# Query and key weights of an attention folded into one matrix ahead of time, in a two-layer Perceiver kernel

## The reference, cut to what matters

```python
# L0_ffn (end of the first layer)
h = layernorm(x, ln1_g, ln1_b)
h = bitlinear(h, w1, b1)          # activations rounded to 8 bits per row, weights to -1, 0, 1
h = gelu(h)                       # 1024 wide
h = layernorm(h, ln2_g, ln2_b)
h = bitlinear(h, w2, b2)
x = x + h
# L1_xattn (start of the second layer), q = layernorm(x), k = v = ctx_1024
wq = einsum('bsd,ed->bse', q, Wq) + bq
wk = einsum('bsd,ed->bse', k, Wk) + bk
wv = einsum('bsd,ed->bse', v, Wv) + bv
att_score = einsum('bqd,bkd->bqk', wq, wk) / 16 + att_mask
x = x + einsum('bqk,bkd->bqd', softmax(att_score), wv)
```

## Time and profile before

| | |
|---|---|
| median of 3 runs | 1007.73 us (1007.71 to 1008.43) |
| the profiled execution | 1003.05 us, its span 1001.0 us |
| PE busy in the span | 905.0 us (90%) |
| VectorE, ScalarE, GpSimd busy | 604.5, 479.5, 105.7 us (60%, 48%, 11%) |
| mean granted TensorE clock in the span | 0.964 |

### The profile page before, as it was taken

One profiled execution on the slowest core, in us unless ns is written; L12 is line 12 of the kernel. 1 busy time (PEld: TensorE's weight loads), 2 busy tenths in 40 slices (PEclk: granted clock), 3 DMA queues, 4 the chain that ended last, 5 costly groups with the idle time before them and its releaser, 6 DMA issues.

```text
span 1001.0 us, 15431 instructions
## 1 busy us (share of the span) xinstructions
PE 905.0 (90%) x6066; PEld 540.6 (54%) x6068; DVE 604.5 (60%) x1075; ACT 479.5 (48%) x951; POOL 105.7 (11%) x118
## 2 busy tenths in 40 slices
PE   6786799999999999999998899588999989988788
PEld 3444444444555555455544677354875854555656
DVE  3876577787885447888843586858414127188240
ACT  2232366777775557777788532225213110676111
POOL 1421011111000000000000200101000007155000
PEclk9999899999999999999999999779999989999889
DMA  9772823445323112222522700705438350000000
GB/s 358 218 202 93 259 79 107 133 127 163 101 66 105 33 32 65 64 67 74 191 96 76 261 1 1 253 25 184 163 133 303 118 168 1 1 1 2 0 1 22
DMA packets 68837, 108.70 MB, mean 109 GB/s; under 512 B 7062, under 2 KB 42902, under 8 KB 66838
## 3 DMA queue, kind: packets, MB, share of 16 engines
q1 hardware_dynamic: 67372, 101.92, 32.0%
q10 hardware_dynamic: 1392, 5.77, 1.4%
HBM read 93.77 MB, written 13.89 MB: 108 GB/s over the span
## 4 chain that ended last, share of the span: by engine, by line
PE 79%; DVE 8%; ACT 7%; issue 3%; DMA 2%; SPq 0%; POOL 0%; ACTq 0%; DVEq 0%
PE psum L1803 13%; PE psum L1785 11%; PE psum L1756 10%; PE psum L2172 6%; PE psum L2145 5%; PE psum L1934 5%; PE psum L1738 5%; PE psum L1728 4%; PE psum L2265 4%; PE psum L1947 3%; ACT arena L748 3%; DVE arena L1100 2%; PE psum L2313 2%; PE psum L2401 1%; PE psum L2298 1%
## 5 line engine op out<-in xcount | busy, mean ns | idle before, releaser
L1100 DVE TENSOR_REDUCE arena<-psum 128x1 f32<-128x1024 f32 x256 | 300.5, 1218 | 111.6 <-PE psum L1756 111.5
L748 ACT ACTIVATE arena<-psum 128x512 f32<-128x512 f32 x512 | 264.7, 604 | 63.4 <-PE psum L1785 62.3
L1785 PE MATMUL psum<-arena 99*128 99x256 bf16 x1024 | 161.0, 275 | 10.4 <-ACT arena L748 4.8
L1756 PE MATMUL psum<-arena 96*128 96x512 bf16 x512 | 152.2, 383 | 18.1 <-DVE arena L1100 11.4
L1785 PEld LDWEIGHTS psum<-arena 99*128 99x128 bf16 x1024 | 80.0, 97 | 109.2 <-ACT arena L748 50.6
L1803 PE MATMUL psum<-arena 128*32 128x256 f32 x2048 | 136.8, 385 | 0.0
L1803 PEld LDWEIGHTS psum<-arena 128*32 128x32 f32 x2048 | 53.5, 109 | 75.5 <-ACT arena L748 36.9
L1728 PE MATMUL psum<-arena 128*128 128x512 f32 x128 | 64.2, 630 | 5.6 <-DMA arena<-ctxT 5.6
L1756 PEld LDWEIGHTS psum<-arena 96*128 96x128 bf16 x512 | 49.3, 99 | 35.7 <-DVE arena L1100 18.8
L1738 PE MATMUL psum<-arena 128*128 128x256 f32 x256 | 64.2, 395 | 1.0 <-ACT arena L726 1.0
L647 POOL TENSOR_TENSOR arena<-arena 128x512 bf16<-128x512 f32 x34 | 41.5, 1221 | 210.0 <-DVE arena L1086 202.3
(11 more groups left out here) (241 smaller groups left out, 967.2 us busy)
## 6 DMA issues: line engine op xcount, KB each, us to landing
arena<-kparts SPq DMA_DIRECT2D x192, 128.0 KB, 3.0
kparts<-arena SPq DMA_DIRECT2D x32, 384.0 KB, 3.3
arena<-ctxT SPq DMA_DIRECT2D x21, 512.0 KB, 5.2
arena<-ctx SPq DMA_DIRECT2D x2, 4096.0 KB, 15.3
arena<-mask SPq DMA_DIRECT2D x8, 1024.0 KB, 5.1
arena<-mask ACTq DMA_DIRECT2D x4, 1024.0 KB, 13.4
arena<-ctxT SPq DMA_DIRECT2D x1, 4096.0 KB, 13.7
arena<-ctxT SPq DMA_DIRECT2D x4, 1024.0 KB, 8.6
```

The lines of the kernel that those rows point to most:

```text
L748: nc.scalar.activation(PR[step % 4][:, pair * CH:(pair + 1) * CH], ring_bank(slot), ACT.Exp)\
L1100: nc.vector.tensor_reduce(MX[g % 2][:, col:col + 1], unit_banks(n).rearrange("p b n -> p (b n)"), AX.X, ALU.max).then_inc(s_maxed, 1)
L1756: last = nc.tensor.matmul(out, q, KST[g % 2][0:ROWS, j, at], start=True, stop=not masked, skip_group_check=True)
L1785: last = nc.tensor.matmul(ring_heads(slot)[:, u, :], KST[gg % 2][0:KROWS, j, kc * P:(kc + 1) * P], QST[0:KROWS, G * g + j, b * S:(b + 1) * S],
```

## The change

The product of the query weights with the key weights is made once, on the chip, and the query's normalised tokens are multiplied by that alone. `fold_key_weights` computes WQ1'WK1 (four fp32 products, 256 columns each), the two bias vectors WK1'bq and WQ1'bk (eight products of one column), and the number bq'bk (two of one by one). ScalarE copies them (`copy_key_weights`, four activations). `project_queries` and `copy_queries` go, for both batches. `fold_queries` reads the tokens `HTE` and the folded weights; `copy_folded` gets a bias operand. `bias_queries` reads the tokens and gets one more product per tile, which adds the number: six products in place of four. The query weights are now loaded untransposed, by a DMA of the same size.

```diff
-        QUERY_BANKS = ((0, 1), (7, 3))
         QC_BANKS = ((2, 3), (7, 3))
-        QE = f32(32768, 1024).rearrange("p (c n) -> p c n", c=CT)
+        WQK = f32(32768, 512).rearrange("p (c f) -> p c f", c=CT)
+        FOLDED = f32(33280, 5)
...
-            load(WQ1, by_part("wq1T"), "l1w_loaded")
+            load(WQ1, by_part("wq1"), "l1w_loaded")
...
-            def copy_queries(b):
-                for f in range(CT):
-                    act.wait_ge(on["e_q"], CT * b + f + 1)
-                    signal(nc.scalar.activation(QE[:, f, batch(b)], psum[:, QUERY_BANKS[b][f], 0:S], ACT.Identity,
-                                                bias=col("bq1", f)), "e_q_copied")
+            def copy_key_weights():
+
+                act.wait_ge(on["e_fold"], 1)
+                signal(nc.scalar.activation(WQK.rearrange("p c f -> p (c f)"), psum[:, 0, :], ACT.Copy), "e_folded")
+                signal(nc.scalar.activation(FOLDED[:, 0:2], psum[:, 1, 0:2], ACT.Copy, scale=D ** -0.5), "e_folded")
+                signal(nc.scalar.activation(FOLDED[:, 2:4], psum[:, 1, 2:4], ACT.Copy), "e_folded")
+                signal(nc.scalar.activation(FOLDED[0:1, 4:5], psum[0:1, 1, 4:5], ACT.Copy), "e_folded")
...
-                    signal(nc.scalar.activation(QC[:, c, batch(b)], psum[:, QC_BANKS[b][c], 0:S], ACT.Copy,
-                                                scale=D ** -0.5), "e_qc_copied")
+                    signal(nc.scalar.activation(QC[:, c, batch(b)], psum[:, QC_BANKS[b][c], 0:S], ACT.Identity,
+                                                scale=D ** -0.5, bias=FOLDED[:, c:c + 1]), "e_qc_copied")
...
             centre_odd(0)
+            copy_key_weights()
+            act.wait_ge(on["e_folded"], 4)
             copy_hidden(0)
             copy_hidden(1)
...
-            copy_queries(0)
             copy_folded(0)
...
-            def project_queries(b):
+            def fold_key_weights():
+
+                for c in range(CT):
+                    for f in range(CT):
+                        nc.tensor.matmul(psum[:, 0, c * 256:(c + 1) * 256], WQ1[:, f, c * P:(c + 1) * P], WK1[:, f, :],
+                                         start=(f == 0), stop=(f == CT - 1), skip_group_check=True)
+                for weights, bias, at in ((WK1, "bq1", 0), (WQ1, "bk1", 2)):
+                    for c in range(CT):
+                        for f in range(CT):
+                            nc.tensor.matmul(psum[:, 1, at + c:at + c + 1], weights[:, f, c * P:(c + 1) * P], col(bias, f),
+                                             start=(f == 0), stop=(f == CT - 1), skip_group_check=True)
                 for f in range(CT):
-                    linear(psum[:, QUERY_BANKS[b][f], 0:S], WQ1, [HTE[:, c, batch(b)] for c in range(CT)], f, "e_q")
+                    last = nc.tensor.matmul(psum[0:1, 1, 4:5], col("bq1", f), col("bk1", f), start=(f == 0),
+                                            stop=(f == CT - 1), skip_group_check=True)
+                last.then_inc(on["e_fold"], 1)
 
             def fold_queries(b):
-                pe.wait_ge(on["e_q_copied"], CT * (b + 1))
                 for c in range(CT):
-                    linear(psum[:, QC_BANKS[b][c], 0:S], WK1, [QE[:, k, batch(b)] for k in range(CT)], c, "e_qc")
+                    linear(psum[:, QC_BANKS[b][c], 0:S], WQK, [HTE[:, k, batch(b)] for k in range(CT)], c, "e_qc")
 
             def bias_queries(b):
                 for i in range(2):
-                    for k in range(CT):
-                        last = nc.tensor.matmul(psum[:, CQ_BANK[b], i:i + 1],
-                                                QE[:, k, (2 * b + i) * P:(2 * b + i + 1) * P], col("bk1", k),
-                                                start=(k == 0), stop=(k == CT - 1))
+                    at = slice((2 * b + i) * P, (2 * b + i + 1) * P)
+                    for c in range(CT):
+                        nc.tensor.matmul(psum[:, CQ_BANK[b], i:i + 1], HTE[:, c, at], FOLDED[:, 2 + c:3 + c],
+                                         start=(c == 0), stop=False, skip_group_check=True)
+                    last = nc.tensor.matmul(psum[:, CQ_BANK[b], i:i + 1], ONES[0:1, :], FOLDED[0:1, 4:5],
+                                            start=False, stop=True, skip_group_check=True)
...
             pe.wait_ge(on["d_hidden"], 4)
+            pe.wait_ge(on["l1w_loaded"], 64)
+            fold_key_weights()
             for i in range(2):
                 turn_hidden(i)
                 project_down(i)
...
-            project_queries(0)
+            pe.wait_ge(on["e_folded"], 4)
             fold_queries(0)
...
-            project_queries(1)
             weigh_context(1, 3)
             fold_queries(1)
```

More of the change, by code:

```diff
@@ L398, in build @@
             d_turned2_copied d_down
-            e_q e_q_copied e_qc e_qc_copied e_cq e_cq_copied e_scores e_masked e_bias e_exp
+            e_fold e_folded e_qc e_qc_copied e_cq e_cq_copied e_scores e_masked e_bias e_exp
             e_turned e_turned_a e_turned_v e_att e_normed e_out
@@ L969, in _ @@
             copy_exps(1, 6)
-            copy_queries(1)
             copy_folded(1)
@@ L2128, in _ @@
             pe.wait_ge(on["x_ready"], 2 * TT + 2)
-            pe.wait_ge(on["l1w_loaded"], 64)
             turn_half(HLE, 0, 2 * TT)
             turned()
-            project_queries(0)
+            pe.wait_ge(on["e_folded"], 4)
             fold_queries(0)
@@ L2467, in layout @@
         "w1T": c(a["L0_ffn_w1"].T), "w2T": c(a["L0_ffn_w2"].T),
-        "wq1T": c(a["L1_xattn_Wq"].T), "wk1": c(a["L1_xattn_Wk"]), "wv1T": c(a["L1_xattn_Wv"].T),
+        "wq1": c(a["L1_xattn_Wq"]), "wk1": c(a["L1_xattn_Wk"]), "wv1T": c(a["L1_xattn_Wv"].T),
         "ctx": c(a["ctx_1024"]), "mask1": c(a["mask_SxS2_ff0"]),
```

## The result

The changed kernel takes 1013.47 us (median of 15 runs, 1009.03 to 1015.65), the kernel before 1007.71 in the same comparison (15 runs). The ratio is 1.006 with a 95% interval of [1.004, 1.008]: slower by 0.6%, some 5.8 us, where 1007.1 had been forecast. The profiled execution took 1013.69 us with a span of 1011.9. The page's shares say almost nothing of the reason.

What follows compares the result with a forecast made beforehand. Bound by a chain of waits across engines up to the scores, then by PE nearly alone. Batch 1's half -1.1, batch 0's -2.5, fold +3.0, clock 0: -0.6 on 1007.73, so 1007.1 us; range 1001.8 to 1010.6.

Steps and rivals of the forecast that it cites:

- the second fetch: Behind the branch, in the fold: starts after three records have run, takes 2.56 us, done at 638.9.
- +3.0: Fold behind the branch: copies end at 646.3, where copy_hidden(0) had started at 643.30; taken from bounds -1.1 to +3.0 us.
- The pieces: Fold behind the branch: three records, a fetch stop, then five wide records 2.4 us, sixteen narrow 3.5, and 0.3.
- ScalarE's copies: Four copies of the fold, ahead of copy_hidden(0) in ScalarE's queue: 1.2 us, ending at 646.3, fold ending at 645.1.
- the delay is carried on in full: From copy_hidden(0) to VectorE's sum at 650.16: steps in a row without slack, so all +3.0 us carries on.
- The gain if the stop were gone: At turn_hidden(0): without its stall, tile 1's transposes start at 644.75 and not 645.85, -1.1 us.
- Batch 0's: Batch 0's half at half clock, up to the scores: one projection fewer, twelve narrow records at 2.6 us; -2.5 us.
- Batch 1's: Batch 1's half at full clock: four products go (1.73 us), bias columns +0.5, copy with bias +0.09; -1.1 us.
- The third rival: Batch 1's half: something else ends last there, so its path isn't shortened; sum +0.5, 1008.2 us, chance 0.03.
- the slower rival: Scores: single columns ahead delay the clock's rise, price 1.5 to 4.1, taken 3.4; 1010.5 us, chance 0.22.
- The other reason for taking 0: Clock at the scores: timed runs lie 4.7 us above the profiled one, so its lucky rise need not be theirs.
- The free fold: Behind the branch: fold ends ahead of 641, turn_hidden(0) goes without stall; -4.7, 1003.0 us, chance 0.35.

Runs made afterwards that it cites:

- e7: Changed kernel with the fold put behind project_down(1) and its copies between two of ScalarE's square roots; 1008.1 us, ratio 1.0028 to the kernel before.
- e6: Kernel before, without the change, its 6 MB mask and context loads held back until tile 1 is rounded; 1004.39 us, ratio 0.9983.
- e1: Kernel before plus the fold and its copies behind the branch, results unused, queries still projected twice; 1012.22 us, ratio 1.0060.
- e2: Changed kernel with PE's part of the fold moved ahead of the branch, behind the mixer's last product; 1008.09 us, ratio 1.0017 to the kernel before.
- e4: Changed kernel with the If's two arms exchanged, so PE falls through into the fold without a taken branch; 1012.29 us, ratio 1.0084 to the kernel before.
- e3: Changed kernel with the 6 MB mask and context loads held back until tile 1 is rounded; 1002.32 us, ratio 0.9976 to the kernel before.
- e8: Changed kernel with the fold ahead of the branch and the mask and context loads held back; 1002.21 us, ratio 0.9956 to the kernel before.
- e11: Changed kernel with the fold ahead of the branch and batch 0's bias columns behind unit 0's scores; 1002.71 us, ratio 0.9981 to the kernel before.
- e9: Changed kernel with fold ahead of the branch, loads held back and batch 0's bias columns behind unit 0's scores; 1003.12 us, ratio 0.9965 to the kernel before.

## Why the prediction was wrong

**The step that failed is the second fetch.** The prediction had it start "on demand" after three records and take 2.56 us, as the first. Its length was nearly right: from the packet to the next record it was 2.67 and 2.52 us here. What was wrong is when it starts. PE wanted it at 641.90, and the packet came at 644.58, 6.24 behind the first. So the code is complete 9.0 us after the mixer's end (638.06 to 647.10), and it was so before (633.64 to 642.55: 8.9). Before, 6.25 of these lay under PE's wait for VectorE, so the stop read 2.18, which was only the part that stuck out. That the second packet fell beside the start of the transposes, 639.98 and 639.89, was a coincidence (and again in e7): in e6 it came 5.65 us ahead of them, and in the changed kernel 2.7 us behind the point where PE needed it. The two packets of the earlier trace rows, 6.3 us apart, were the evidence, and I read them as two separate demands. With 9.0 us and then 5 wide and 16 narrow records and four more, 5.9 us at half clock, the fold ends 15 us after the mixer, and nothing of that piece has cover: +6.3 us instead of +3.0. Of these 3.3 us the code's coming makes 3.8 (9.0 us after the mixer's end in place of the 5.3 of the forecast); the rest of the fold took 0.3 less than reckoned, and the way from it to `copy_hidden(0)` 0.1 less. e1, e2, e4 and e7 show that it is the place behind a taken branch; e3 that the load on the DMA engines nearly doubles the distance of the two pages there.

**The pieces.** Three records, then five, with an "issue" between them: right. Durations of the fold at half clock: 2.50 for five wide records (2.4 forecast), 3.21 for sixteen narrow (3.5): right. ScalarE's copies were forecast to end 1.2 us behind the fold and to push `copy_hidden(0)`. They end under the transposes, at 653.7, and L908 starts at 654.03, right behind the turning, so they cost nothing. That the sum lost little by this is luck: from the fold's end to `copy_hidden(0)` it had 1.2 us for the copies and nothing for the transposes, and the transposes took 1.06:

```profile
653.01 0.60 ACT L920 ACTIVATE arena<-psum 128x512 f32<-128x512 f32 x1 [14.02 <-PE psum L2042]
...
654.03 1.02 ACT L908 ACTIVATE arena<-psum 128x1024 bf16<-128x1024 bf16 x1 [0.29 <-PE psum L2022]
```

**That the delay is carried on in full**: right, 6.3 at `copy_hidden(0)` and at the sum. (The gain if the stop were gone, put at 1.1 us, measured 1.4: the sum at 9.00 in e4, e6 and e8.) It was the step that turned an error of 3.3 us at the fetch into one of 3.3 in the whole.

**The halves.** Batch 0's -2.37 (forecast -2.5, with the twelve narrow records at 2.6 measured as 0.65 + 0.51 + 0.94 + 0.51 = 2.61). Batch 1's -0.86 (forecast -1.1; the twelve narrow records took 1.76, from 751.07 to 752.83, where 1.58 was reckoned). The third rival falls.

**The clock.** I took 0 and made it the slower rival, at 1.5 to 4.1 us. It cost +2.5 under the scores, and the dip at 889 goes with the last +0.9. As an effect the rival was right, and the three pairs with the columns moved speak for its mechanism, as far as said above. Its price would not have saved the number: -0.6 + 3.3 for the fetch + 2.5 + 0.9 + 0.4 for the halves gives the 6.5 of the table. The range ended at 1010.6, since it added the clock to a +3.0 that was given as an upper bound. That bound was none: it held only if the second fetch starts when PE asks. The other reason for taking 0, the 4.7 us between the timed runs and the profiled one, fits the lower clock near 560 us, far ahead of the change, and says nothing of the rise before the scores. (Added up from their pieces the chances come to 0.42 for the same and 0.21 for slower, where the text has 0.41 and 0.22; nothing hangs on it.)

**The free fold**, the first rival, fails here for the same reason, but e2 shows that the fold is free directly ahead of the branch, though the stop at `turn_hidden(0)` stays.

**The rule.** The Trainium skill, "Runtime: NRT & Kernel Launch", "Instruction fetch mechanics", says that a taken branch outside the held pages forces a fetch and that fetching in sequence is mostly hidden. The measurement decides against the second half behind a branch: the sequential page came 6.2 us after the first, while PE stood still for 5.20. Where PE falls through, in e4, the trace agrees: a page comes at 647.98, in the middle of the fold, and there is no stop.

**Left open.** Why the pages behind the mixer come 6.2 us apart under load and 3.3 without it: whether the packets wait for bandwidth or for their turn in a DMA engine's own order wasn't told apart. Why three records run from the first page here, and one in e4 at the start: no run moved the code within its page. What makes the clock fall near 558 us in ten of the thirteen profiles. And e8 is the one version whose interval lies below 1, 0.9956 [0.9917, 0.9995]: 0.4% under the kernel before. Of ten versions that were timed one such interval is weak evidence.

## What to carry over

Behind the taken branch of this kernel PE had the code of three records only until 8.7 to 9.5 us after its last product ahead of it, with the DMA engines full, and until 3.3 us after it with the loads held back. So put behind such a branch what would have to wait anyway, and put free work ahead of it, where the fetch runs beside it. A stop that a trace shows is only the part of a fetch that nothing else covers; read the length from the packets of the fetch queue, and ask what it would be if the cover went. And when wide products are cut to one ahead of a long run of them, look at the clock and at what few-column work stands between: here a saving of 2.4 us at the lower clock was taken back by 2.5 us of the clock's later rise.

## What the hardware showed unexpectedly

The second page behind a branch comes without PE having run what is on the first: at 639.62 in e6, 5.65 us ahead of the first transpose. Its distance to the first page depends on the load and on what stands ahead of the branch. With the mixer's last product there it is 6.2 to 6.3 us under load, whether three fp32 records run between or none (6.23 in e1, 6.24 in e7), and 3.28 and 3.42 without it (e3, e6). With the fold ahead of the branch it is 5.43 and 5.28 under load (e2, e11) and 5.33 and 4.80 without (e8, e9), so there the load hardly matters. The page that the branch needs comes while work ahead of it still runs, with 3.2 us of it left in e2 and 2.8 in e3.

Records of one column with a 128x128 fp32 stationary tile cost 0.20 us each at the lower clock (3.21 for 16) and 0.105 at the full one (1.68 for 16 in e7). The loads of the tile fill that time (PEld busy 0.98 of the 1.00 us from 670 to 671 in the changed kernel), so a record of one column is nearly half as dear as one of 256 (0.22 at the full clock).
